# Layer-1 edge pass of a graph network: attributes loaded by one transfer of 128 partitions, and the chain of state sums issued between the next block's instructions

## The reference

```python
q = (x @ Wq + bq).reshape(n, H, C); k = ...; v = ...      # H = 8 heads, C = 32
e = (edge_attr @ We).reshape(-1, H, C)                    # 100000 edges x 256
k_j = k[src] + e
v_j = v[src] + e
q_i = q[dst]
alpha = jnp.sum(q_i * k_j, axis=-1) / jnp.sqrt(jnp.float32(C))
amax = jax.ops.segment_max(alpha, dst, num_segments=n)
ex = jnp.exp(alpha - amax[dst])
denom = jax.ops.segment_sum(ex, dst, num_segments=n)
out = jax.ops.segment_sum(v_j * (ex / denom[dst])[:, :, None], dst, num_segments=n)
```

## Time and profile before

| | us |
|---|---|
| time, median of 3 runs (5672.48 to 5680.9) | 5678.94 |
| span of the profiled execution | 5673.3 |
| VectorE busy in it | 3824.3 |
| GpSimd busy | 3388.4 |
| TensorE matmul busy | 2860.0 |
| ScalarE busy | 1441.9 |

### The profile page before, as it was taken

One profiled execution on the slowest core, in us unless ns is written; L12 is line 12 of the kernel. 1 busy time (PEld: TensorE's weight loads), 2 busy tenths in 40 slices (PEclk: granted clock), 3 DMA queues, 4 the chain that ended last, 5 costly groups with the idle time before them and its releaser, 6 DMA issues. The chain is left out here.

```text
span 5673.3 us, 49658 instructions
## 1 busy us (share of the span) xinstructions
PE 2860.0 (50%) x13052; PEld 2232.1 (39%) x13052; DVE 3824.3 (67%) x6117; ACT 1441.9 (25%) x2526; POOL 3388.4 (60%) x3382
## 2 busy tenths in 40 slices
PE   7513200000000000015899986888888888884777
PEld 5412200000000000014677633777776777673456
DVE  7357778786454545546543464989899998995763
ACT  1113333332233333311222211222222222221320
POOL 0267777777777777753440276777777777773200
PEclk9655555555555555556799998999999999896888
DMA  3133344432363333323232355999999999993114
GB/s 101 36 84 108 107 130 148 130 104 83 103 220 110 109 110 109 110 87 124 93 124 68 107 191 191 317 319 323 319 319 321 319 323 318 323 318 113 67 47 148
DMA packets 290231, 961.79 MB, mean 170 GB/s; under 512 B 79248, under 2 KB 119831, under 8 KB 248468
## 3 DMA queue, kind: packets, MB, share of 16 engines
q0 software_dynamic: 171296, 483.60, 28.6%
q1 hardware_dynamic: 118788, 476.59, 24.9%
HBM read 626.03 MB, written 345.69 MB: 171 GB/s over the span
## 5 line engine op out<-in xcount | busy, mean ns | idle before, releaser
L1249 PE MATMUL e_psE<-e_we,e_eaT 128*128 128x256 f32 x3136 | 903.5, 415 | 279.3 <-DVE e_wv L1148 179.3
L1111 POOL DMA_INDIRECT e_kv<-kv,rec x784 | 875.7, 1117 | 266.3 <-issue 253.7
L779 POOL DMA_INDIRECT g_g<-t,rec x784 | 777.1, 991 | 254.0 <-issue 253.7
L779 POOL DMA_INDIRECT g_g<-t,dst_of x784 | 743.6, 949 | 259.3 <-issue 257.2
L1249 PEld LDWEIGHTS e_psE<-e_we,e_eaT 128*128 128x128 f32 x3136 | 649.4, 210 | 400.7 <-ACT e_eaT L1192 299.4
L1407 PE MATMUL j_psM<-ident,tail 128*128 128x128 f32 x32 | 7.2, 416 | 1149.0 <-PEq L53 1149.0
L1250 PE MATMUL e_psE<-e_kv,ident 128*128 128x256 f32 x1568 | 509.8, 409 | 0.0
L816 DVE TENSOR_TENSOR_SCAN g_wv<-g_fx,g_wv 128x2176 f32<-128x2176 f32 x98 | 459.0, 4684 | 0.2 <-issue 0.2
L1407 PEld LDWEIGHTS j_psM<-ident,tail 128*128 128x128 f32 x32 | 6.8, 322 | 1149.8 <-issue 1149.8
L1118 POOL DMA_INDIRECT e_q<-q,q_of x392 | 370.9, 946 | 119.7 <-issue 119.7
L956 ACT ACTIVATE g_st<-g_wv 128x2048 f32<-128x2048 f32 x98 | 375.9, 3836 | 0.0
(11 more groups left out here) (519 smaller groups left out, 6620.8 us busy)
## 6 DMA issues: line engine op xcount, KB each, us to landing
state<-e_st SPq DMA_DIRECT2D x98, 1088.0 KB, 6.2
e_ea<-in_edge_attr SPq DMA_DIRECT2D x98, 896.0 KB, 9.8
state_f<-g_st SPq DMA_DIRECT2D x49, 1088.0 KB, 4.4
state_b<-g_st SPq DMA_DIRECT2D x49, 1088.0 KB, 4.3
m_work<-xs SPq DMA_DIRECT2D x119, 128.0 KB, 2.3
ys<-m_work SPq DMA_DIRECT2D x119, 128.0 KB, 1.7
xs<-g_ta SPq DMA_DIRECT2D x28, 512.0 KB
g_g<-t,rec POOLq DMA_INDIRECT x784
```

The costliest lines, as they stand in the source:

```text
L779: pool.indirect_dma_start(g[:, u, j, :], None, tab, bass.IndirectOffsetOnAxis(ap=at_, axis=0)).then_inc(gat[u], 16)
L1111: pool.indirect_dma_start(kv[:, u, b, :], None, c.kv, bass.IndirectOffsetOnAxis(ap=c.rec[:, t, 1:2], axis=0)).then_inc(gkv[u][b // 4], 16)
L1249: nc.tensor.matmul(half, eaT[:, m, j, k, :], we[:, k, :], start=(k == 0), stop=False)
```

## The change

**Attributes in one transfer.** The first 432 columns of each of the 128 partitions (`EARLY` = 432, 54 blocks) lie inside the attribute array for every partition, so they are now loaded from it by one transfer of 128 partitions. The other 352 columns of all partitions are copied to `ea_late` during the layer-0 passes, in 44 pieces of 127 partitions x 8 KB (blocks 18 to 61, two transfers each), and one more for the last partition: 46 MB in place of 12.8 MB. The load of a block runs one block further ahead.

**VectorE.** The body of a block issues the chain of the block before between its own instructions; each `drain` is replaced by a wait on a semaphore that the earlier instruction counts. The sum over channels is two instructions of 1024 elements in place of one of 2048, the second half of the values is added later, and `wv` has two buffers. ScalarE writes the exponentials a second time, into the PSUM tile `pw`, and the weighing instruction reads them from there. The chain of the last block stands alone at the end.

**The others.** TensorE transposes the next block's attributes between the two halves of a block's products, over 3 PSUM banks in place of 4, so that its fourth group of transposes waits for ScalarE's first copy, which ScalarE makes after the exponentials. GpSimd gathers 4 rows of `kv`, then `q`, then the other 4, with a wait ahead of each.

```diff
-            def load_attributes(b, u):
+            def load_attributes(b, u, late):
-                    sp.dma_start(ea[0:112, u, :, :], rows(A["edge_attr_256"][0:112 * T, :])).then_inc(eg[u], 16)
-                    sp.dma_start(ea[112:P, u, :, :], rows(c.ea_tail)).then_inc(eg[u], 16)
+                    if late:
+                        rows = c.ea_late[:, bass.ds(b * (B * D) - EARLY * D, B * D)]
+                    else:
+                        rows = bass.AP(A["edge_attr_256"].tensor, 0, [[T * D, P], [1, EARLY * D]])[:, at_]
+                    sp.dma_start(ea[:, u, :, :], rows).then_inc(eg[u], 16)
...
# SP, layer-0 passes, one piece of the copy
+                at_ = slice(a * B * D, (a + 1) * B * D)
+                for p0, p1 in slices_of(0, P - 1):
+                    late = bass.AP(ea.tensor, (p0 * T + EARLY) * D, [[T * D, p1 - p0], [1, real * D]])
+                    sp.dma_start(c.ea_late[p0:p1, at_], late[:, at_]).then_inc(other, 16)
...
# GpSimd
                 if blk >= U:
-                    pool.wait_ge(used, blk - U + 1)
+                    pool.wait_ge(ed, 4 * (blk - U) + 6)
                     c.alone(pool)
+                keys_and_values(blk, 0)
                 if blk >= U:
-                    pool.wait_ge(q_used, blk - U + 1)
+                    pool.wait_ge(logits, 3 * (blk - U + 1))
...
+                if blk >= U:
+                    pool.wait_ge(ed, 4 * (blk - U) + 8)
+                keys_and_values(blk, 1)
...
# VectorE, after; step(b) is chain(n - 1, 1 - u, b)
+            def chain(n, u, b):
+                if b == 0:
+                    v.wait_ge(free, n + 1)
+                    v.wait_ge(weighed, n + 1)
+                else:
+                    v.wait_ge(chained, n * (B - 1) + b)
+                nc.vector.scalar_tensor_tensor(
+                    out=st[:, u, b, 0:D], in0=st[:, u, b - 1, 0:D] if b else before[:], scalar=kept[:, u, b:b + 1],
+                    in1=wv[:, u, b, :], op0=ALU.mult, op1=ALU.add).then_inc(std if b == B - 1 else chained, 1)
...
+                step(7)
+                v.wait_ge(scanned, 2 * n + 2)
+                tt(ex[:], at[:], top[:], ALU.subtract).then_inc(exd, 1)
+                values(1)
...
-                    tt(weighed, weighed, cw[:, :, 1:B1].rearrange("p h b -> p b h").unsqueeze(3).to_broadcast([P, B, H, C]),
-                       ALU.mult)
+                tt(products, products, pw.rearrange("p h b -> p b h").unsqueeze(3).to_broadcast([P, B, H, C]),
+                   ALU.mult).then_inc(weighed, 1)
...
# ScalarE
+            def one_block(n, u, more, turned):
+                keep_state(n - 1, 1 - u)
+                act.wait_ge(std, n)
+                if more:
+                    mark_segments(n + 1, 1 - u)
+                powers(n)
+                if turned:
+                    transposed_attributes(n + 2, u)
...
# TensorE
+            def one_block(blk, u, gathered, next_loaded):
+                pe.wait_ge(gkv[u][0], gathered)
+                for m in range(2):
+                    keys_with_attributes(blk, u, m)
+                if next_loaded is not None:
+                    turn(blk + 1, 1 - u, next_loaded, True)
+                pe.wait_ge(gkv[u][1], gathered)
+                for m in range(2, 4):
+                    keys_with_attributes(blk, u, m)
```

More of the change, by code:

```diff
@@ L1085, in store, with ahead @@
                              st[:, u, :, :]).then_inc(so[u], 16)
-                sp.wait_ge(so[1 - u], (i + 1) * 16)
+                sp.wait_ge(so[1 - u], older * 16)
                 sp.sem_inc(free, 1)
-            load_attributes(0, 0)
-            load_attributes(1, 1)
-            with sp.Fori(0, NBLK // U - 1) as i:
-                for u in range(U):
-                    sp.wait_ge(tp, (i * U + u + 1) * 4)
-                    c.alone(sp)
-                    load_attributes(i * U + u + U, u)
-                    store(i, u)
-            store(NBLK // U - 1, 0)
-            store(NBLK // U - 1, 1)
+            def ahead(blk, u, older, late):
+                sp.wait_ge(tp, blk * 4 + 8)
+                c.alone(sp)
+                load_attributes(blk + 3, 1 - u, late)
+                store(blk, u, older)
+            load_attributes(0, 0, False)
+            load_attributes(1, 1, False)
+            sp.wait_ge(tp, 4)
+            c.alone(sp)
+            load_attributes(2, 0, False)
+            ahead(0, 0, 1, False)
+            direct = EARLY // B // U - 2
+            for first, end, late in ((0, direct, False), (direct, NBLK // U - 2, True)):
+                with sp.Fori(first, end) as i:
+                    ahead(i * U + 1, 1, i + 1, late)
+                    ahead(i * U + 2, 0, i + 2, late)
+            store(NBLK - 3, 1, NBLK // U - 1)
+            store(NBLK - 2, 0, NBLK // U)
+            store(NBLK - 1, 1, NBLK // U)
             sp.wait_ge(so[1], (NBLK // U + 1) * 16)
@@ new lines, in _ @@
+            one_block(0, 0, nrows, False)
+            with v.Fori(0, NBLK // U - 1) as i:
+                one_block(i * U + 1, 1, (i + 1) * nrows, True)
+                one_block(i * U + 2, 0, (i + 2) * nrows, True)
+            one_block(NBLK - 1, 1, NBLK // U * nrows, True)
+            chain(NBLK - 1, 1, 0)
+            denominators(NBLK - 1, 1)
+            for b in range(1, B):
+                chain(NBLK - 1, 1, b)
+            v.wait_ge(std, NBLK)
+            v.wait_ge(act_mt, NBLK)
@@ new lines, in turn @@
+            def turn(blk, u, loaded, reused):
+                pe.wait_ge(eg[u], loaded)
+                for m in range(4):
+                    if m == 3:
+                        pe.wait_ge(tcp, blk * 4 + 1)
+                    elif reused and m == 0:
+                        pe.wait_ge(tcp, blk * 4)
+                    for j in range(2):
+                        for k in range(2):
+                            o = (2 * j + k) * P
+                            last = nc.tensor.transpose(psT[m % 3][:, o:o + P], ea[:, u, 2 * m + j, k * P:(k + 1) * P],
+                                                       c.ident[:])
+                    last.then_inc(tp, 1)
```

240 lines of the change are left out of this document (127 added, 113 removed).

## The result

The changed kernel takes 5599.28 us (median of 4 runs, 5596.16 to 5603.79), beside 5679.28 us for the kernel before on the same chip. The ratio is 0.9859 with a 95% interval of 0.9847 to 0.9871, so it is faster by 1.4%, 80 us. The forecast was 5571 us in a range of 5540 to 5630: the sign and the range hold, and the gain is 28 us smaller than forecast.

What follows compares the result with a forecast made beforehand. VectorE was taken to set 16.57 us a block, with GpSimd close at 16.4. 98 blocks falling to 15.4 gain 114.7 us, less 4.4 and 2 us lost: net 108 us, from 5679 to 5571 us, range 5540 to 5630.

Steps and rivals of the forecast that it cites:

- What bounds the kernel before: Layer-1 pass: VectorE sets 16.57 us a block, GpSimd follows at 16.4, and both must fall.
- VectorE after: VectorE per block: 14.95 us busy falls to 14.1, plus 0.2 of gaps, 14.3 us; bounds 13.9 and 16.4.
- GpSimd after: GpSimd's gathers per block: 15.0 us plus 0.4 of short stalls, 15.4 us; bounds 15.0 and 16.4.
- The forecast's other estimate: GpSimd's short stalls per block: what 1.37 us leaves beside the stall under the weighing, at most about 0.3 us.
- The ends: Outside the block period: last chain alone loses 4.4 us, the copy in the layer-0 passes 2 us.
- The stall's cause: Weighing with both operands in SBUF stalls a gather, 2.31 us and not 0.94; one PSUM operand ends the long stall.
- The DMA engines: Transfers per block need about 13.6 us, or 14.8 with slow attribute loads, both under 15.4; merged transfer costed at nothing.
- rival (c): Slower: TensorE's clock drops in two idles, a ring of 19.3 us closes, VectorE waits; 5761 us, chance 0.07.
- I take full clock: TensorE: table load leaves the loop and 3.0 us of idle are split, so full clock; ring 13.6 us, under 15.4.
- (a): Semaphores cost what drains did: VectorE stays at 16.4 us, 5669 us; chance 0.13 of somewhere in 15.7 to 16.4.
- (b): DMA engines are the bound after all, rate staying near 321 GB/s: 16.6 us a block, 5685 us, chance 0.07.
- (d): GpSimd at its floor, 15.0 to 15.2 us a block: 5532 to 5552 us, chance 0.13.

Runs made afterwards that it cites:

- e2: Kernel before, with the exponentials also written to PSUM and read there by the weighing, 3 transpose banks; order and drains kept: 5681.42 us, ratio 1.0008.
- e1: Changed kernel with the second copy of the exponentials, `pw`, in SBUF and not in PSUM: 5829.67 us, ratio 1.0267.
- e17: Changed kernel, its order and semaphores kept, with 13 drains of VectorE a block added: 5731.33 us, ratio 1.0089.
- e15: Changed kernel with each chain step cut to 32 of 256 channels, so its result isn't the reference's: 5530.48 us, ratio 0.9739.
- e10: e1 with the product for the carried state moved behind the weighing: 5722.09 us, ratio 1.0075.
- e14: e9 with the second addition of values moved up between the scan of `mt` and the seventh chain step: 5606.10 us, ratio 0.9866.
- e7: Kernel before with the attributes in one transfer of 128 partitions and the copy of 33 MB it needs: 5676.65 us, ratio 0.9997.
- e3: Changed kernel with the attributes loaded by two transfers again, partitions 0 to 111 and 112 to 127: 5596.22 us, ratio 0.9851.
- e4: Changed kernel with 11 gathers a block, not 12, from the third block on, so its result isn't the reference's: 5482.27 us, ratio 0.9653.
- e9: Changed kernel with the product for the carried state taking its factor from PSUM, `pw` widened to nine columns: 5579.21 us, ratio 0.9830.

## Why the prediction was right, and where it was off

**What bounds the kernel before: right, shown.** VectorE at 16.57 with GpSimd close behind. e2 takes the stall away and gains nothing, e1 takes the drains away and keeps the stall, and loses. One count was off: the code before has 14 drains for each block and not 13 (seven in the chain, two ahead of the denominators' scan, and one behind each of the copy, the values, the sum and the two scans of the maximum). At the forecast's 0.08 us of overlap the one more is 0.1 us a block.

**VectorE after: 14.3 us forecast, not reached as a bound.** Its busy time is 13.6 us a block, 0.5 under the forecast of 14.1, with idle 0.0 ahead of the chain steps; the waits cost nothing, as forecast. In e17 it is 430.10 / 500 x 17.0 = 14.6, 1.0 more, which agrees with the 13 x 0.08 of overlap; the other 0.5 us were gained by the new order itself and not by the missing drains, and weren't taken apart. It showed nowhere in the time, since GpSimd is the bound. The gap that the forecast gave a drain, 0.06 us, was too small: seven steps have six gaps between them, 0.07, and the group of the window gives 0.08.

**GpSimd after: the bound, and its size was off.** This is the term of the sum that failed: "I take 0.4: 15.4 us". It measured 15.63, of which e15 shows 0.69 above its own 14.94. The forecast spread a layer-0 excess of 0.12 us over a share of the time. A hold is in fact set by what is left of the instruction under which the gather starts: 0.27 us left of L1246 gave 1.09 us (4011.94 above), 1.08 left of the weighing gave 1.89 (e10), and 1.50 left gave 2.31, each time 0.81 or 0.82 us more than what was left, where a gather that isn't held takes 0.95. A gather that starts right behind the start of the instruction can go free: those that start up to 0.08 us behind the start of the first step of a chain take 0.95 us after the change, and those that start 0.14 to 0.18 us behind it take 1.13 to 1.17 in e14. The gather at 4009.01 had 0.41 left of the step and 0.62 to the end of the scan behind it, and took 1.38. So a start under a chain step costs up to 0.43 us, where I had 0.12. The forecast's other estimate, what the kernel before leaves beside the long stall, was no guide either: the steps cost 0.19 us a block in the old order and 0.59 in the new one. The 0.23 us make 98 x 0.23 = 22.5 of the 28 us.

**The ends: off by some 6 us.** The pass's first store starts at 3556.4, where it was 3549.2, and from the last store's start to the span's end it is 5594.4 - 5072.2 = 522.2 us, where it was 5673.3 - 5156.3 = 517.0. That is 12.4 us together, of which the forecast had 6.4. The part ahead of the pass wasn't taken apart. The first store of e7, which has the copy and the old order, starts at 3552.1; in the runs that go on from the change it starts between 3554.5 and 3567.2, so a few us of this term are scatter.

**The stall's cause: right, shown by e1 against after** (same order, one operand moved, 230 us). The Trainium skill, in "SBUF — State Buffer", section "Who interferes with whom", says that VectorE with two SBUF inputs contends with GpSimd instructions that read SBUF, and infers that descriptor generation is spared, since it needs the write interface. The first half agrees with every trace here. The inference doesn't: gathers are held by a `tensor_tensor`, by 2.37 us in e1.

**The DMA engines: right.** e3 and e7 show that the merged transfer changes no time. The Trainium skill's rule in "DMA: Bandwidth & Descriptors", section "Rules for kernel authors", for one transfer of 128 partitions fits what it does for the engines' share (0.93 against 1.02, 0.90 against 1.00) at no gain in time in this kernel.

**The clock and rival (c): mostly right.** The granted clock is 0.94 in the window, up from 0.91. It still drops behind some waits for gathers, as in this row of the changed kernel, where a group of four matmuls takes 2.08 us in place of 1.03, and in the window around it, where the granted clock is 0.50:

```profile
4007.90 2.08 PE L1349 MATMUL e_psE<-e_we,e_eaT 128*128 128x256 f32 x4 [3.18 <-DMA e_kv<-kv,rec]
```

```profile
4007.90:4010.50 2.60, 2.60 (x6) 2.16 (x7) 2.60 (x6) 0.00 (x0) 2.18 (x2) 0.50 0.95 334
```

So the forecast's sign of being wrong, idles of TensorE above 3 us with a clock of 0.5, did show: 31 such idles between 3600 and 5050 us, against 27 before. "I take full clock" was too good, though the clock stood at 0.5 for less time, 166 of these 1450 us against 256. It costs nothing as long as GpSimd is the bound, and in the window GpSimd never waits. The forecast had no term for these half-clock stretches; that they needed none was luck. The table load is gone from the loop.

**The rivals.** (a) fell by e4 and by the idle of 0.0, (b) by e7 with the rates of e4 and e15, (c) by the run of the change itself. (d), GpSimd at its floor, is what e15 reached with most of the chain's work left out. Two sums don't come out of their own terms: (b) at 16.6 us gives 5688 us and not 5685, and "0.60 + 0.13 + most of (a)" is at most 0.86 and not 0.89.

**The other signs.** The attributes (9.0 to 9.2 us), the DMA share and the table load came as written. Gathers of `kv` have a mean of 1.03 us and not 0.95 to 1.0, and 65 gathers take over 1.3 us where none was to; the forecast would have read another cause from that, but it is the same cause, under chain steps with a scan behind them. VectorE is busy 87% of the window and not 92%.

## What to carry to other kernels

When one engine holds another and both are near the bound, price them together: either edit alone gave 0 (e2) or a loss of 150 us (e1), and both gave 80 us gained. A stall that depends on where one engine's start falls in another's instruction is priced by the time left in that instruction, for each start in a block, and not by a mean excess from another stage. Once GpSimd's gathers are the bound, look at each VectorE instruction with two SBUF operands for one that can come from PSUM; a factor that ScalarE writes anyway is cheap (16 us for one changed operand of 256 elements, e9).

## What the runs showed of the hardware that I hadn't expected

- A gather of 128 rows issued by GpSimd is held by the VectorE instruction under which it starts, if that has two operands in SBUF, and then by such a one that follows without a gap. In the 13 traces of kernels with full chain steps, 3600 to 5050 us, 6695 gathers start under an instruction with one operand in PSUM, a reduction or a copy, and none of them takes over 0.97 us. Starting 0.02 us behind the weighing's own start it took 0.95 us (e10), and 0.14 us behind the start of L1246 it was held through the weighing that followed, 3.32 us in all (e1). A scan of 72 elements behind a chain step prolongs the hold too, to 1.38 us; the next chain step behind that scan doesn't.
- A drain with a semaphore wait behind it costs more than the gap in the old chain tells: 0.26 us each in e17, where the old chain has 0.08 of gap and the earlier trace rows 0.08 of overlap.
- A DMA share of 1.00 was no bound: the same traffic at the same time went with a share of 0.90 (e7).
